# Packed attention-and-expert steps: all four probability tiles turned by VectorE and transfers, and a new order of the products

## The reference, cut to what matters

```python
q = rmsnorm(x @ Wq, gq); k = rmsnorm(ctx @ Wk, gk); v = ctx @ Wv      # per head, 128 wide
attn = softmax(q @ k.T / sqrt(128)); x = x + tanh(g) * (attn @ v) @ Wo  # summed over 16 heads
gate, up = xs @ Wg[e].T, xs @ Wu[e].T                                   # expert e, 352 wide
out = (silu(gate) * up) @ Wd[e].T * w                                   # 4 experts for each of 512 rows
```

## Time and profile before

| | |
|---|---|
| median of 3 runs | 1406.72 us (1406.38 to 1410.99) |
| the profiled execution | 1406.11 us, its span 1404.3 us |
| TensorE busy | 1376.5 us, 98% |
| VectorE, ScalarE, GpSimd busy | 1140.6 us (81%), 976.5 (70%), 942.4 (67%) |
| TensorE's granted clock | 0.998 |
| DMA | 204.59 MB, mean 146 GB/s |

### The profile page before, as it was taken

One profiled execution on the slowest core, in us unless ns is written; L12 is line 12 of the kernel. 1 busy time (PEld: TensorE's weight loads), 2 busy tenths in 40 slices (PEclk: granted clock), 3 DMA queues, 4 the chain that ended last, 5 costly groups with the idle time before them and its releaser, 6 DMA issues.

```text
span 1404.3 us, 23125 instructions
## 1 busy us (share of the span) xinstructions
PE 1376.5 (98%) x7614; PEld 1175.1 (84%) x7614; DVE 1140.6 (81%) x2072; ACT 976.5 (70%) x2165; POOL 942.4 (67%) x729
## 2 busy tenths in 40 slices
PE   8899999999999999999999999999999999999998
PEld 6778778888888888888888888888888888877886
DVE  7888778788888888887878888887878787888777
ACT  7863467788876767667676767667676766666764
POOL 4876557777776567667676767676776757776561
PEclk9999999999999999999999999999999999999999
DMA  9420023333433555656564646566565653442312
GB/s 338 156 78 16 23 75 107 106 117 116 122 113 113 167 167 183 190 168 193 176 200 156 204 160 189 183 179 188 174 198 163 189 170 125 138 145 94 98 61 90
DMA packets 135734, 204.59 MB, mean 146 GB/s; under 512 B 10112, under 2 KB 70528, under 8 KB 135616
## 3 DMA queue, kind: packets, MB, share of 16 engines
q1 hardware_dynamic: 131856, 190.79, 42.7%
q0 software_dynamic: 3760, 12.32, 3.3%
HBM read 157.72 MB, written 45.35 MB: 145 GB/s over the span
## 4 chain that ended last, share of the span: by engine, by line
PE 76%; DVE 3%; POOL 2%; ACT 2%; DMA 1%; issue 1%; SPq 0%; ACTq 0%; POOLq 0%
PE j_bank L578 9%; PE j_bank L580 9%; PE j_bank L579 9%; PE w_bank L578 8%; PE w_bank L580 8%; PE w_bank L579 8%; PE s_bank L578 4%; PE s_bank L580 3%; PE s_bank L579 3%; PE t_bank L655 3%; PE t_bank L613 2%; PE t_bank L578 1%; PE t_bank L579 1%; PE t_bank L580 1%; PE w_bank L761 1%
## 5 line engine op out<-in xcount | busy, mean ns | idle before, releaser
L1032 ACT ACTIVATE prob<-s_bank,neg_bias,q_scale 128x512 f32<-128x512 f32 x255 | 197.4, 777 | 141.5 <-DVE neg_bias L1545 141.5
L1613 DVE SCALAR_TENSOR_TENSOR x_sb<-w_bank,inv_sum,x_sb 128x512 f32<-128x512 f32 x254 | 186.7, 745 | 32.0 <-PE w_bank L580 30.9
L1947 POOL TENSOR_TENSOR xnT_lo<-xnT_raw,xnT_hi 128x512 fp32r<-128x512 f32 (+2 forms) x47 | 126.4, 2691 | 63.1 <-ACT xnT_hi L990 63.1
L1524 DVE TENSOR_REDUCE neg_max<-s_bank 128x1 f32<-128x512 f32 x255 | 168.0, 679 | 0.9 <-PE s_bank L580 0.9
L578 PE MATMUL j_bank<-wkv_lo,cT_hi 128*128 128x256 f32 x512 | 145.0, 283 | 0.0
L1947 POOL TENSOR_TENSOR cT_round<-cT_raw,x_round 128x1408 fp32r<-128x1408 f32 (+1 forms) x31 | 104.4, 3367 | 59.9 <-ACT x_round L990 59.9
L580 PE MATMUL j_bank<-wkv_hi,cT_lo 128*128 128x256 f32 x512 | 144.4, 282 | 0.0
L579 PE MATMUL j_bank<-wkv_hi,cT_hi 128*128 128x256 f32 x512 | 144.2, 282 | 0.0
L1988 POOL TENSOR_TENSOR q_scale<-q_ss,minus_half 128x4 f32<-128x4 f32 x64 | 66.0, 1031 | 106.3 <-DVE q_ss L1537 106.3
L1947 POOL TENSOR_TENSOR sqs_lo<-xn,sqs_hi 128x512 fp32r<-128x512 f32 x62 | 104.0, 1677 | 34.5 <-ACT xn L1120 33.8
L1580 DVE STREAM_TRANSPOSE prob<-prob 128x1024 f32<-128x1024 f32 x59 | 73.5, 1245 | 60.8 <-ACT prob L1032 60.4
(11 more groups left out here) (312 smaller groups left out, 4600.2 us busy)
## 6 DMA issues: line engine op xcount, KB each, us to landing
turn<-prob SPq DMA_DIRECT2D x59, 512.0 KB, 3.1
prob<-turn SPq DMA_DIRECT2D x236, 128.0 KB, 3.2
stage<-w SPq DMA_DIRECT2D x96, 256.0 KB, 3.5
xnT_raw<-w_gu SPq DMA_DIRECT2D x31, 704.0 KB, 4.5
cT_raw<-w_gu SPq DMA_DIRECT2D x31, 704.0 KB, 5.9
xnT_raw<-w_dn SPq DMA_DIRECT2D x16, 768.0 KB, 5.4
cT_raw<-w_dn SPq DMA_DIRECT2D x15, 768.0 KB, 5.4
planes<-bits SPq DMA_DIRECT2D x16, 512.0 KB, 5.0
```

What stands on the lines that cost most here:

```text
L1032: nc.scalar.activation(dst, src, ACT.Exp, bias=neg_bias[:, u % 2, i:i + 1], scale=q_scale[:, u % 2, i:i + 1], accum_out=row_sum[:, u % 2, ...
L1524: nc.vector.tensor_reduce(neg_max[:, u % 2, i:i + 1], score_bank(t, i)[:], AX_X, ALU.max, negate=True).then_inc(own_max, 1)
L1613: nc.vector.scalar_tensor_tensor(out=here, in0=w_bank[0][:] if packed else out_bank(t, i)[:], scalar=inv_sum[:, w % 2, i:i + 1], in1=here, ...
L1947: return nc.gpsimd.tensor_tensor(dst, src, hi, ALU.subtract)
```

## The change

In packed steps tiles 2 and 3 become a second moved pair (`both_moved`): a second VectorE transposition, store, four loads, a cast on ScalarE and a subtraction on VectorE. The first pair's cast and subtraction move to the head of the next step, the subtraction from VectorE to GpSimd. TensorE's eight transpositions a step for tiles 2 and 3 go away. The copy of key rows 2 and 3 moves from VectorE to ScalarE. The value product goes behind `key_value(1)` and into `t_bank[1]`; the output products use `w_bank[0]` and `t_bank[1]` by turns. The down weights go ahead of the store of the block before and of `store_pair`; the second pair's store goes ahead of the next gate and up weights. In steps 4 to 15 the late tile is turned by VectorE and transfers too, and its subtraction goes to GpSimd one step later. The diff, cut to its core:

```diff
 def turned_tiles(u):
+    if both_moved(u):
+        return ()
...
         def out_bank(t, i):
+            if in_block(t):
+                return (w_bank[0], t_bank[1])[i % 2]
...
+            def store_second(u):
+                sp.wait_ge(p_quads, PAIRS_MOVED[u] + 2)
+                wait(sp, second_moved, 16 * NT * SECONDS[u])
+                sp.dma_start(turn_dram[3:5].rearrange("i p m -> p i m"), prob_pair(1)).then_inc(p_stored, 16)
+            def load_second(u):
+                sp.wait_ge(p_stored, 16 * (PAIRS_MOVED[u] + 2))
+                for c in range(NT):
+                    sp.dma_start(prob[c * QUAD:(c + 1) * QUAD, 2:4, :]..., turn_dram[3:5]...[c]).then_inc(second_moved, 16)
+            def store_late(t):
+                sp.wait_ge(late_turned, n + 1)
+                sp.dma_start(turn_dram[2], late_row(t)).then_inc(late_stored, 16)
+            def load_late(t):
+                sp.wait_ge(late_stored, 16 * (t - LATE_HEAD + 1))
+                for c in range(NT):
+                    sp.dma_start(late_row(t)[c * QUAD:(c + 1) * QUAD, :]..., turn_dram[2]...[c]).then_inc(late_moved, 16)
...
                 if 0 <= b < NB:
                     gate_up_weights(b, 1, e)
+                if in_block(t):
+                    down_weights(b, e)
                 if 0 < b <= NB:
                     y_store(b - 1)
                 if in_block(t):
                     store_pair(t - 1)
-                    down_weights(b, e)
                     load_pair(t - 1)
...
                 if not in_block(t):
+                    store_late(t)
                     store_pair(t - 1)
                     load_pair(t - 1)
+                    load_late(t)
...
+                store_second(t - 1)
                 if 0 <= b < NB - 1:
                     gate_up_weights(b + 1, 0, e)
+                load_second(t - 1)
...
@@ TensorE, steps outside the block @@
                     key_value(0, (1,))
-                    late_turn()
                     key_value(1)
...
@@ TensorE, packed step @@
                 project_down()
                 if down:
                     query_squares()
-                values()
                 key_value(0)
                 gate_up(0)
+                key_value(1)
+                values()
                 scores(2)
-                key_value(1)
-                project_out(0)
                 scores(3)
                 query((0, 1))
+                project_out(0)
+                gate_up(1)
                 project_out(1)
-                probs(2)
-                gate_up(1)
-                project_out(2)
                 key_turn()
                 query((2, 3))
+                project_out(2)
                 turn_inner()
-                probs(3)
                 project_out(3)
...
@@ ScalarE, packed step @@
                     gate_up_hi(0)
                     rows_to_hi()
+                    moved_hi(w)
+                    moved_second_hi(w)
                     ...
-                    values_hi()
+                    first_rows()
                     softmax(0)
                     softmax(1)
-                    first_rows()
+                    gate_up_hi(1)
                     gate_tanh(0)
-                    gate_up_hi(1)
+                    second_rows()
+                    key_squares()
+                    values_hi()
+                    values_rows()
                     softmax(2)
-                    key_squares()
-                    values_rows()
                     softmax(3)
-                    probs_hi(2)
                     next_wkv()
+                    down_hi()
                     gate_tanh(1)
-                    down_hi()
                     key_hi()
                     query_hi()
                     inner_hi()
-                    moved_hi(u)
                     query_squares()
-                    probs_hi(3)
...
@@ VectorE, packed step @@
                     maximum(0)
                     maximum(1)
+                    gate_up_lo()
+                    rows_to_lo()
+                    squares_out()
                     inverses()
-                    gate_up_lo()
-                    squares_out()
-                    rows_to_lo()
-                    copy_y()
+                    moved_second_lo(w)
                     shift(0)
                     shift(1)
-                    values_lo()
+                    copy_y()
                     turn_quads()
                     inner(0)
                     maximum(2)
                     shift(2)
-                    second_rows()
-                    add(0)
+                    values_lo()
                     maximum(3)
                     shift(3)
+                    add(0)
+                    turn_second()
+                    inner(1)
                     add(1)
-                    probs_lo(2)
-                    inner(1)
-                    add(2)
                     key_lo()
                     query_lo()
+                    add(2)
                     inner_lo()
                     add(3)
-                    moved_lo(u)
-                    probs_lo(3)
...
@@ GpSimd @@
                 def moved_lo(v):
+                    pool.wait_ge(pair_hi, PAIRS_MOVED[v] + 1)
+                    if up:
+                        pool.wait_ge(a_lo, b + 1)
                     lower(probT_pair(1), prob_keys(), f32(probT_pair(0))).then_inc(pair_lo, 1)
...
                     take_rows(b + 1)
-                if not in_block(t - 1):
-                    moved_lo(w)
+                moved_lo(w)
                 query_scale()
...
                 gate_up_lo()
+                late_lower(t - 1)
                 scale_keys()
```

More of the change, by code:

```diff
@@ L93 @@
 LATE_HEAD = min(LATE)
+LATE_NEEDED = {next(t for t, item in enumerate(ITEMS) if item[1] == b): NT * b for b in range(1, B)}
 XN, XNS = numbered("df", ACT_ORDER)
@@ L152 @@
 MOVES = [sum(moved(v) for v in range(u)) for u in range(NI + 1)]
+SECONDS = [sum(both_moved(v) for v in range(u)) for u in range(NI + 1)]
+PAIRS_MOVED = [m + n for m, n in zip(MOVES, SECONDS)]
 def flamingo_kernel(nc, x, xT, ctxT, vecs, w0, bits, w1, w_gu, w_dn, topk_idx, topk_w, x0_dram, rows_dram, y_dram, turn_dram, out):
@@ L663, in values @@
                     wait(pe, pair_lo, MOVES[w + 1])
+                    wait(pe, second_lo, SECONDS[w + 1])
                     need(pe, v_lo, 1, w, 1)
@@ L684, in project_out @@
                         need(pe, o_lo, 1, w, 2)
-                    if t in LATE and i == 1:
-                        pe.wait_ge(late_lo, t - LATE_HEAD + 1)
                     if i == 0:
-                        if not packed:
-                            need(pe, o_lo, 1, w, 1)
+                        need(pe, o_lo, 1, w, 1)
                         if fresh(w):
@@ L698, in project_out @@
                     else:
-                        need(pe, w_added, 4, w, i if packed else i - 1)
-                    product(w_bank[0][:] if packed else out_bank(t, i)[:], [a[:, i * P:(i + 1) * P] for a in oT],
+                        need(pe, w_added, 4, w, i - 1)
+                    product(out_bank(t, i)[:], [a[:, i * P:(i + 1) * P] for a in oT],
                             [a[:] for a in wo]).then_inc(w_mm, 1)
@@ L809, in project_down @@
                     last.then_inc(d_mm, 1)
-                def late_turn():
-                    if t not in LATE:
-                        return
-                    pe.wait_ge(late_normed, t - LATE_HEAD + 1)
-                    need(pe, w_added, 4, w, 0)
-                    for j in range(DT):
-                        last = pe.transpose(w_bank[1][:, j * P:(j + 1) * P], late_row(t)[:, j * P:(j + 1) * P], ident[:])
-                    last.then_inc(late_turned, 1)
                 def key_values():
@@ L1613, in add_of @@
                     nc.vector.scalar_tensor_tensor(
-                        out=here, in0=w_bank[0][:] if packed else out_bank(t, i)[:], scalar=inv_sum[:, w % 2, i:i + 1],
+                        out=here, in0=out_bank(t, i)[:], scalar=inv_sum[:, w % 2, i:i + 1],
                         in1=here, op0=ALU.mult, op1=ALU.add).then_inc(w_added, 1)
@@ L2055, in squares_lo, with late_lower @@
                     lower(sqs[1][:], squares(t), f32(sqs[0][:])).then_inc(sq_lo, 1)
+                def late_lower(v):
+                    if v not in LATE:
+                        return
+                    pool.wait_ge(late_hi, v - LATE_HEAD + 1)
+                    lower(late_tile(1, v), late_blocks(v), f32(late_tile(0, v))).then_inc(late_lo, 1)
                 if t == 0:
```

114 lines of the change are left out of this document (75 added, 39 removed).

## The result

The changed kernel takes 1469.07 us (median of 4 runs, 1462.79 to 1473.32) where the kernel before, beside it on the same chip, takes 1408.33: ratio 1.042, 95% interval 1.040 to 1.045. It is slower by 60 us; 1386 was predicted, and 1402 was the upper end. The profiled execution took 1473.32 us, span 1471.5.

What follows compares the result with a forecast made beforehand. TensorE alone was taken to bound the kernel, busy through each 22.58 us packed step. From 1406.11 us, 31 x (0.99 gain - 0.50 refill wait) + 5.3 for late turns = 20.5 gave 1386 us, range 1370 to 1402.

Steps and rivals of the forecast that it cites:

- the 0.44 of a late turn: Late steps: taking four transpositions and the delay behind them off TensorE gains 0.44 us each, 5.3 us over 12.
- the 0.99: Packed steps: TensorE gains 0.79 us from transpositions and 0.20 at the head, from 22.58 to an ideal 21.59.
- The head wait for the lower part of the queries: Head of a packed step: TensorE's 0.37 us wait for the queries' lower part shrinks, gaining 0.2 us.
- L - 4.9: First output product waits for the refill's landing time minus 4.9 us: 0 or 1.0 by buffer, mean 0.5 a step.
- lands L later: 4.5 for one buffer, 5.9 for the other.: Refill of gate and up weights: lands 4.5 us after issue in one buffer, 5.9 in the other, alternating.
- GpSimd's pair subtraction 2.4 and its query scale 1.0: A + 6.6.: Chain behind ScalarE's cast of the refill: GpSimd's subtraction and query scale end 6.6 us after that cast starts.
- the rule as a rival: Pair subtractions of VectorE and GpSimd exclude each other: VectorE stands 0.25 us a step, 1393 us; chance 0.1.
- the store issue takes 0.4.: SP's queue: issuing the second pair's store delays the next weights' issue by 0.4 us.
- The weight loads behind the four loads go 1.8 us later: Late steps, SP's queue: weights issued 1.8 us later behind the four loads; cost taken as 0.
- The refill gives all back: Second store's bytes keep refill landings at 5.9 us, wait 1.0 a step, 1401 us; chance 0.15.
- The slower case: SP's queue behind the second store delays the refill loop; decides from landings of 6.2 us, 1426 at 6.7; chance 0.13.
- No waits: Refill lands in 4.5 to 4.9 us, so packed steps gain fully: step 21.6, total 1370 us; chance 0.2.

Runs made afterwards that it cites:

- e6: Changed kernel with the attention weights issued ahead of the four late loads in early steps: 1459.40 us, ratio 1.036.
- e10: Kernel before plus only the late tiles turned by VectorE and transfers, attention weights issued ahead of the late loads: 1405.13 us, ratio 0.997.
- e15: Changed kernel with the late tiles of steps 4 to 15 back on TensorE, second run of this edit: 1440.83 us, ratio 1.024.
- e14: e7 with the second pair's store and loads left out, so its quarters stay unmoved: 1401.94 us, ratio 0.994.
- e4: Changed kernel with the second pair's store and loads cut to a quarter of their bytes: 1437.58 us.
- e12: Kernel before plus copies of 512 KB ahead of the refill and 4 x 128 KB behind it, nothing waiting for them: 1416.98 us, ratio 1.006.
- e13: e15 with the second pair's store and loads left out, so its quarters stay unmoved: 1423.03 us, ratio 1.010.
- e5: Changed kernel with SP reading the next expert's number ahead of the second store's wait: 1465.45 us, ratio 1.041.
- e8: e7 with SP also reading the next expert's number early, as in e5: 1454.15 us, ratio 1.033.
- e3: Changed kernel with VectorE's second-pair subtraction moved behind shift(1): 1459.31 us.
- e7: Changed kernel, late tiles on TensorE, ScalarE casting the first pair before the weights, VectorE subtracting it, GpSimd the second pair, a_lo wait gone: 1431.64 us, ratio 1.017.
- e9: Kernel before plus only the late tiles turned by VectorE and transfers: 1414.24 us, ratio 1.004.
- e2: Changed kernel with the next gate and up weights issued ahead of the second pair's store: 1489.82 us.
- e1: Changed kernel with the late tiles of steps 4 to 15 back on TensorE, first run of this edit: 1448.99 us.
- e16: The changed kernel run once more, unedited, against the kernel before: 1463.60 us, ratio 1.040.

## Why the prediction was wrong

**The bound and the gain.** That TensorE alone set the end was right. What leaves it in a late step was sized well: e6 shows the 0.44 of a late turn as 0.43 a step, e10 as 0.3. In the packed steps less than the 0.99 is to be seen: at full clock TensorE is busy 21.9 us of a step in e15 and 22.0 in e14, against 22.58 before and an ideal of 21.59. Part of that is the slower first matmul behind a wait (0.50 us at 780.44, 0.39 at 801.58 in the earlier trace rows). The head wait for the lower part of the queries stands in no list of waits of the changed kernel; what that gave (0.2) was not isolated.

**The walk.** Its structure stood: the refill loop, the wait for oT_lo, ScalarE's waits for w_gu. I predicted a wait of L - 4.9 in every other step. Measured, the loop is 18.3 to 18.5 plus L against an ideal of 21.6, so every landing over about 3.2 us makes a wait, and the shortest seen is 4.2. Three terms were mis-sized, and by the table they make the whole step, 0.85 + 0.79 + 0.98 = 2.6 on 21.9:

- *"lands L later: 4.5 for one buffer, 5.9 for the other."* I took the landings from a kernel that had none of the second pair's bytes, in the paragraph after writing that 1 MB is added. And I misread them: the medians of the earlier trace rows mix the refill with the second halves. Before, the refill alone landed after 5.07 in one buffer and 4.73 in the other; what told its landings apart more was the attention-weight loads issued just ahead of it, 4.3 us with none, 4.6 with one, 5.8 with two. Changed, L was 5.99: by the same loads, 5.4 us with none, 5.8 with one, 6.8 with two. So the long landings came mostly in every third step and not in every other. e4, e12 and e13 show the bytes in it, 0.5 to 1.5 us. The Trainium skill (DMA: Bandwidth & Descriptors, section "Queues, rings and completion order") says that a DMA engine takes a ring's descriptors in order; e5 and e8 are in line with it, where a refill issued 0.6 us closer behind the store took 0.1 and 0.9 us longer from its issue.
- *"GpSimd's pair subtraction 2.4 and its query scale 1.0: A + 6.6."* 2.4 was right to the row. The query scale took 2.10, since VectorE's pair subtraction, which I had placed at the same moment, lay beside it: 1.05 us in each step (e3, e7). I had the rule as a rival, but priced the wrong partner: VectorE standing for GpSimd, 0.25 us, chance 0.1. The softmaxes hang on GpSimd here.
- *"the store issue takes 0.4."* Between the store and the refill SP reads the expert's number: 1.17 us from issue to issue. Taken alone this term buys next to nothing back (e5), since the store then goes out later and the landing takes longer.

**The late weights.** *"The weight loads behind the four loads go 1.8 us later ... I take 0, because ScalarE has over a microsecond of idle time."* The 1.8 was right (1.9 measured). But they also landed behind 256 KB more, ScalarE stood up to 3.8 us for them, and 5.3 gained became 5.0 lost: what I called idle time was less than that, and I had read no row of it. e6, e9 and e10 show this step alone.

**The rivals.** *The refill gives all back* (0.15) had the landing right, 5.9 against 5.99 measured, and named its cause, the store's bytes; it fell on the chain. The slower case (0.13) was the right mechanism, the loop through SP's queue behind the second store, but its point, L = 6.2, was computed with the chain 1.8 us too short. *No waits* fell as well. Of the signs named for being right, the transpositions went as announced, 536 to 288 of t_bank<-ident,prob. Of those for being wrong, the late steps got longer; the value product did not wait for the second pair, except where e2 and e3 made it.

**The sum again.** 31 x (24.52 - 22.09) = 75.3 for the packed steps and 10.3 for the late ones (5.3 + 5.0), from 1386: 1472, against 1473.3 measured. The share of the lower clock lies inside these pieces and wasn't tried by itself.

**How the loss divides.** Steps, one cause at a time: changed 24.52 (24.41 again), late tiles back 23.53 (23.85 in e1), no second transfers 23.03, swapped as well 22.4, before 22.57. So 0.6 to 1.0 comes with the late part, by L and SP's queue; the way from the one to the other stays open. The second pair's transfers come to 0.5 net of the gather's collision, and the collision of the power with the a_lo wait to 0.6. The causes aren't independent: between e7 and e14 the transfers cost 1.0, and even the last step of this ladder gains only 0.2.

## What to carry to other kernels

When an order is moved so that a transfer's landing feeds the next issue of the same transfer, price the whole loop, and price the landing with the bytes that the change adds, since from then on every 0.1 us is paid in every step. Two operations of VectorE and GpSimd that a walk puts at one moment have to be asked which of them stands and who hangs on it. In a queue that works in order, put what is needed soonest first: here that one move made 9 us of difference and turned the late part from a loss into the only gain.

## What was not expected of the hardware

- A refill issued 0.6 us closer behind a 512 KB store took longer from its issue: in the swapped order L went from 5.75 to 6.61 us, and the kernel lost 22 us (e8); in e5 it was 0.1 to 0.2 us and nothing lost.
- A small GpSimd operation, a power of 128 x 4, goes from 1045 to 2100 ns beside a 1.21 us VectorE subtraction, and a gather issued by GpSimd from 1.05 to 2.4 us behind the start of a 1.61 us one (e13).
- Packed steps with the same instructions had landings of 5.22 (e15) or 5.89 us (e16) in the mean, where only the steps before them differed. The cause stays open.
- Waits for landings came with a lower TensorE clock as well: five stretches at the lower level in the packed steps of the changed kernel, each behind idle time, and none in e15.
